# A two-batch gated cross-attention block on one core: the order of five instruction queues is written anew

## The reference, cut to what matters

```python
def _L0_xattn_ref(x1, x2, x1_scale, x1_zp, x2_scale, x2_zp):
    q1 = fake_quant(x1, x1_scale, x1_zp)     # clip(round(x/s + z), 0, 255), then (q - z) * s
    q2 = fake_quant(x2, x2_scale, x2_zp)
    return jnp.matmul(q1, q2)                # (2, 1024, 2048) x (2, 2048, 2048)

def _L0_ffn_ref(x, route_w, A, Bw):          # 8 experts of rank 16, top 1
    logits = jnp.einsum('bsd,ed->bse', x, route_w)
    topk_v, topk_idx = jax.lax.top_k(logits, 1)
    route_weight = jax.nn.one_hot(topk_idx[..., 0], E) * topk_v
    h = jnp.einsum('bsd,erd->bser', x, A)
    return jnp.einsum('bser,eor->bso', route_weight[..., None] * h, Bw)

x = x + jnp.tanh(g_xattn[0]) * _L0_xattn_ref(_layernorm(x), ctx_4096, ...)
x = x + jnp.tanh(g_ffn[0]) * _L0_ffn_ref(_layernorm(x), route_w, A, Bw)
```

## Time and profile before

| what | value |
|---|---|
| median of 3 runs | 368.99 us (368.56 to 371.08) |
| profiled execution, its own time | 369.88 us |
| its span, first to last instruction | 367.8 us (2.08 lie outside) |
| mean granted TensorE clock | 0.996 |
| TensorE busy | 336.4 us, 91% |
| VectorE / ScalarE / GpSimd busy | 262.0 / 197.2 / 174.0 us |
| main queue's DMA (q1) | 87.11 MB, 80.3% of 16 engines |

### The profile page before, as it was taken

How to read it: one execution, slowest core, us unless ns; L and a number is a source line. 1 busy time by engine, 2 the same in 40 slices (tenths; PEclk the granted TensorE clock), 3 DMA queues, 4 the chain that set the end, 5 groups by cost and what they waited for, 6 DMA issues and landing times.

```text
span 367.8 us, 5879 instructions
## 1 busy us (share of the span) xinstructions
PE 336.4 (91%) x2262; PEld 187.0 (51%) x2262; DVE 262.0 (71%) x553; ACT 197.2 (54%) x129; POOL 174.0 (47%) x199
## 2 busy tenths in 40 slices
PE   0249999999999989999999999999999999999983
PEld 0124544555666644645564645555465546464851
DVE  3899784698876984879539688775885768365853
ACT  1699589458994382282999554406054305104360
POOL 2386649501207534137799537425426181505281
PEclk9999999999999999999999999999999999999998
DMA  7999989959768969997699997578919864913836
GB/s 309 398 365 386 396 326 313 342 223 362 244 215 218 220 229 168 401 344 161 174 262 253 218 367 150 155 145 317 199 26 279 215 124 82 211 44 58 268 134 228
DMA packets 93906, 87.63 MB, mean 238 GB/s; under 512 B 71844, under 2 KB 72868, under 8 KB 89764
## 3 DMA queue, kind: packets, MB, share of 16 engines
q1 hardware_dynamic: 93856, 87.11, 80.3%
q10 hardware_dynamic: 12, 0.00, 0.0%
HBM read 52.49 MB, written 16.78 MB: 188 GB/s over the span
## 4 chain that ended last, share of the span: by engine, by line
PE 61%; DMA 12%; DVE 9%; ACT 8%; issue 4%; POOL 3%; SPq 1%; ACTq 0%; DVEq 0%
PE main L1575 39%; DMA stage<-in_ctx 7%; ACT c L735 3%; DMA xs<-in_x 3%; DVE bn L971 3%; PE hp L1617 3%; PE outp L1658 3%; PE outp L1660 3%; PE outp L1659 3%; PE hp L1614 3%; PE hp L1613 3%; DMA prow<-in_g_ffn 2%; PE turn L1503 1%; ACT yn L782 1%; POOL yn L586 1%
## 5 line engine op out<-in xcount | busy, mean ns | idle before, releaser
L1575 PE MATMUL main<-q,qa 128*128 128x512 bf16 x864 | 196.8, 382 | 1.2 <-POOL q L593 0.8
L1575 PEld LDWEIGHTS main<-q,qa 128*128 128x128 bf16 x864 | 83.4, 98 | 100.1 <-issue 2.9
L586 POOL TENSOR_TENSOR yn<-y,yn 128x2048 f16<-128x2048 f32 x13 | 53.0, 4079 | 31.5 <-ACT y L788 31.2
L735 ACT ACTIVATE c<-stage,zpc,inv 128x2048 int8<-128x2048 f32 x24 | 49.7, 2088 | 19.5 <-DMA stage<-in_ctx 19.3
L1104 DVE SCALAR_TENSOR_TENSOR xs<-main,cc,xs 128x512 f32<-128x512 f32 x45 | 33.5, 744 | 31.2 <-PE main L1575 30.6
L593 POOL CAST q<-c 128x2048 bf16<-128x2048 int8 x24 | 45.1, 1900 | 9.1 <-ACT c L735 8.7
L574 POOL TENSOR_SCALAR ve<-mv 128x1 f32<-128x1 f32 x16 | 3.1, 192 | 91.3 <-DVE mv L1137 87.3
L793 ACT ACTIVATE whT<-wp 128x256 f16<-128x256 f16 x16 | 6.1, 379 | 67.5 <-PE wp L1646 67.5
L971 DVE BATCH_NORM_STATS2 bn<-xs 128x6 f32<-128x512 f32 x52 | 32.0, 678 | 10.9 <-DMA xs<-in_x 10.9
L1184 DVE SCALAR_TENSOR_TENSOR xs<-outp,tsc,xs 128x512 f32<-128x512 f32 x44 | 31.1, 736 | 11.5 <-PE outp L1660 11.4
L1613 PE MATMUL hp<-WT,yT 128*128 128x136 f16 x256 | 34.8, 223 | 0.0
(11 more groups left out here) (132 smaller groups left out, 440.4 us busy)
## 6 DMA issues: line engine op xcount, KB each, us to landing
stage<-in_ctx SPq DMA_DIRECT2D x24, 1024.0 KB, 7.7
xs<-in_x SPq DMA_DIRECT2D x13, 1024.0 KB, 6.4
out<-xs SPq DMA_DIRECT2D x12, 1024.0 KB, 4.9
yT<-in_ctx SPq DMA_DIRECT2D x4, 1024.0 KB, 11.2
y<-in_ctx SPq DMA_DIRECT2D x4, 1024.0 KB, 11.4
c<-in_x SPq DMA_DIRECT2D x3, 1024.0 KB, 8.3
out<-c SPq DMA_DIRECT2D x3, 1024.0 KB, 5.1
c<-in_L_ffn_A SPq DMA_DIRECT2D x1, 1024.0 KB, 16.7
```

The costliest lines, as they stand in the source:

```text
L586: pool.tensor_tensor(yn[:, 1, :], y[:, :], yn[:, 0, :], ALU.subtract).then_inc(s_ylo_made, 1)
L735: act.activation(c8_of(piece), place(piece), ACT.Identity, bias=zpc[:, 1:2], scale=inv[:, 1:2])\
L1575: last = pe.matmul(bank_of(n)[:, :], q1T(t)[:, k, :], q2[:, nb, k, :], start=(k == 0), stop=(k == KC - 1))
```

## The change

The five written-out lists get a new order; functions, buffers, semaphores and their counts, `RAMP`, `HOME` and the split between engines stay. The same calls are made, each as often as before. What moves: x2 loads behind pieces 0 and 1, x3, A and the router behind pieces 4 to 7 (before: behind 1 and 3); in blocks 0 and 1 the runs of tiles 0 to 2 go piece by piece over several tiles, instead of unit by unit; tile 3's transposes come after those 24 runs. From there to the end many neighbours in each list change places. The core of the diff, in the order SyncE, GpSimd, ScalarE, VectorE, TensorE:

```diff
             load_x(0)
             load_x(1)
-            load_x(2)
             load_ctx(0)
             load_ctx(1)
-            load_x(3)
+            load_x(2)
             load_ctx(2)
             load_ctx(3)
-            load_a()
-            load_router()
             load_ctx(4)
             load_ctx(5)
             load_ctx(6)
             load_ctx(7)
+            load_x(3)
+            load_a()
+            load_router()
+            load_ctx(8)
             load_x(4)
-            load_ctx(8)
             load_ctx(9)
...
             flip_high(3)
+            flip_low(3)
             load_x(6)
-            flip_low(3)
+            load_ctx(25)
             store(1)
-            store(2)
             flip_high(4)
             flip_low(4)
+            store(2)
+            load_ctx(26)
             load_x(7)
-            load_ctx(26)
             load_ctx(27)
+            flip_high(5)
             store(3)
+            flip_low(5)
+            load_x(8)
             load_ctx(28)
-            load_x(8)
             load_ctx(29)
-            flip_high(5)
-            flip_low(5)
-            store(4)
             flip_high(6)
             flip_low(6)
             flip_q1(8)
+            store(4)
+            load_ctx(30)
             load_x(9)
-            load_ctx(30)
             load_ctx(31)
...
             store(7)
-            load_x(13)
-            load_x(14)
             flip_high(10)
             flip_low(10)
             flip_q1(12)
+            load_x(13)
+            load_x(14)
...
             first_norm(0)
             first_norm(1)
-            first_norm(2)
             widen_ctx(0)
             widen_ctx(1)
-            first_norm(3)
+            first_norm(2)
             widen_ctx(2)
...
+            second_norm(6)
             first_norm(8)
-            second_norm(6)
+            low_rows(6)
             widen_x(8)
-            low_rows(6)
             widen_ctx(16)
...
+            affine_first(0)
             affine_first(1)
-            affine_first(0)
+            affine_ctx(0)
             affine_x(1)
-            affine_ctx(0)
             affine_ctx(1)
+            affine_ctx(2)
             affine_x(2)
-            affine_ctx(2)
             affine_ctx(3)
-            affine_x(3)
             affine_ctx(4)
-            mult_a()
             affine_ctx(5)
             affine_ctx(6)
             affine_ctx(7)
+            affine_x(3)
+            mult_a()
             affine_ctx(8)
...
             norm_full(2)
+            affine_x(5)
             take_wh(0)
-            affine_x(5)
...
             take_q1T(0, 0)
+            take_q1T(0, 1)
             see_q1(0)
-            stats1(2)
-            take_q1T(0, 1)
             widen_x(1)
             see_q1(1)
-            stats1(3)
-            widen_x(2)
+            stats1(2)
             take_q1T(1, 0)
             take_q1T(1, 1)
-            scale_a()
-            scale_router()
+            widen_x(2)
+            take_q1T(2, 0)
+            take_q1T(2, 1)
+            see_q1(2)
             unit_terms(0, 0)
...
+            add_main(2, 0)
...
+            stats1(3)
+            scale_a()
+            widen_x(3)
+            see_q1(3)
             take_q1T(3, 0)
             take_q1T(3, 1)
+            add_main(0, 1)
+            scale_router()
             take_a(0)
...
+            add_main(3, 2)
             take_b(0)
             take_b(1)
+            unit_terms(0, 3)
             take_b(2)
             take_b(3)
-            add_main(3, 2)
-            unit_terms(0, 3)
             scale_b()
             add_main(0, 3)
...
+            add_experts(3, 0)
             take_q1T(6, 1)
...
+            stats1(7)
             add_experts(3, 1)
...
+            gate(6)
+            add_experts(5, 0)
             stats1(9)
-            gate(6)
             tile_terms(8)
             add_main(8, 0)
...
+            stats1(13)
+            stats1(14)
             tile_terms(12)
-            add_experts(8, 3)
+            add_main(12, 0)
...
             stats2_sum(15)
+            add_experts(12, 1)
+            norm_group(15, 0)
+            norm_group(15, 2)
             add_experts(12, 2)
-            norm_group(15, 0)
             add_experts(12, 3)
-            norm_group(15, 2)
             gate(14)
...
             turn_q1(0, 0)
             turn_q1(0, 1)
+            main(0, 0, 0)
             turn_q1(1, 0)
             turn_q1(1, 1)
-            column_sums(0, [0])
-            main(0, 0, 0)
+            main(0, 0, 1)
+            main(1, 0, 0)
+            main(1, 0, 1)
+            main(0, 0, 2)
+            main(1, 0, 2)
             turn_q1(2, 0)
             turn_q1(2, 1)
-            main(0, 0, 1)
...
+            main(1, 1, 0)
+            main(1, 1, 1)
+            main(2, 1, 0)
+            main(2, 1, 1)
+            main(1, 1, 2)
+            main(2, 1, 2)
+            main(0, 1, 0)
+            main(0, 1, 1)
+            main(0, 1, 2)
...
             turn_q1(3, 0)
             turn_q1(3, 1)
             turn_a(0)
-            column_sums(0, [1])
-            main(0, 1, 0)
-            main(0, 1, 1)
+            main(3, 0, 0)
+            main(3, 1, 0)
+            main(3, 1, 1)
             turn_a(1)
...
             turn_y(15, 2)
             h_group(15, 0)
+            h_group(15, 1)
+            turn_y(15, 3)
             expert_product(14, 0)
-            turn_y(15, 3)
             expert_product(14, 1)
-            h_group(15, 1)
```

More of the change, by code:

```diff
@@ L453, in _ @@
             load_ctx(18)
+            load_x(5)
             load_ctx(19)
-            load_x(5)
             load_ctx(20)
@@ L522, in _ @@
             flip_low(14)
+            store(10)
             store(11)
@@ L632, in _ @@
             widen_ctx(11)
-            widen_x(4)
+            first_norm(4)
             widen_ctx(12)
@@ L637, in _ @@
             widen_ctx(15)
+            widen_x(4)
             second_norm(0)
@@ L863, in _ @@
             affine_ctx(16)
+            affine_x(4)
             affine_ctx(17)
@@ L891, in _ @@
             norm_full(4)
+            affine_ctx(24)
+            affine_ctx(25)
+            take_wh(3)
             affine_x(6)
-            affine_ctx(24)
-            take_wh(3)
-            affine_ctx(25)
+            norm_high(5)
+            norm_full(5)
             affine_ctx(26)
+            affine_x(7)
             affine_ctx(27)
-            norm_high(5)
             take_wh(4)
-            affine_x(7)
-            norm_full(5)
-            affine_x(8)
             norm_high(6)
             norm_full(6)
+            affine_x(8)
             widen_ctx(18)
@@ L934, in _ @@
             norm_high(11)
+            norm_full(11)
             affine_x(13)
-            norm_full(11)
+            affine_x(14)
             take_wh(10)
-            affine_x(14)
             norm_high(12)
             norm_full(12)
+            affine_x(15)
             take_wh(11)
@@ L943, in _ @@
             norm_full(13)
-            affine_x(15)
             take_wh(12)
@@ L1338, in _ @@
             add_main(5, 1)
+            add_experts(2, 2)
+            add_experts(2, 3)
+            gate(4)
             add_main(5, 2)
+            add_main(5, 3)
             take_q1T(6, 0)
+            stats2_sum(5)
+            tile_terms(6)
+            add_experts(3, 0)
             take_q1T(6, 1)
-            add_main(5, 3)
-            stats2_sum(5)
-            add_experts(3, 0)
+            stats1(7)
             add_experts(3, 1)
@@ L1366, in _ @@
             add_main(7, 1)
+            add_experts(4, 1)
+            add_experts(4, 2)
+            add_experts(4, 3)
             add_main(7, 2)
@@ L1423, in _ @@
             add_experts(9, 1)
-            add_experts(9, 2)
-            add_experts(9, 3)
-            add_main(12, 0)
-            add_main(12, 1)
             add_main(12, 2)
@@ L1430, in _ @@
             stats2_sum(12)
+            add_experts(9, 2)
+            add_experts(9, 3)
             tile_terms(13)
@@ L1756, in _ @@
             main(2, 3, 2)
-            main(2, 3, 3)
+            spread_scales()
+            turn_q1(4, 0)
+            turn_q1(4, 1)
             turn_y(0, 0)
             turn_y(0, 1)
+            main(2, 3, 3)
+            h_group(0, 0)
             column_sums(3, [3])
+            turn_y(0, 2)
+            turn_y(0, 3)
             main(3, 3, 0)
@@ L1795, in _ @@
             expert_product(0, 3)
+            h_rows_high(2)
+            turn_q1(5, 0)
+            main(4, 2, 3)
+            h_rows_low(2)
             turn_wh(1)
-            h_rows_high(2)
-            h_rows_low(2)
-            main(4, 2, 3)
-            expert_product(1, 0)
             main(4, 3, 0)
@@ L1882, in _ @@
             main(7, 3, 1)
+            expert_product(4, 3)
+            turn_wh(5)
             main(7, 2, 2)
@@ L1938, in _ @@
             h_rows_low(8)
+            expert_product(7, 2)
             column_sums(10, range(NB))
             main(10, 0, 0)
+            main(10, 1, 0)
+            main(10, 1, 1)
```

(18 more changed lines are left out.)

451 lines of the change are left out of this document (199 added, 252 removed).

## The result

The changed kernel takes **364.05 us** (median of 3 runs, 363.53 to 364.25) against 368.99: a ratio of 0.987, 95% interval 0.9844 to 0.9897. In another set of runs it was 363.46 us, ratio 0.9869 (0.9849 to 0.9888). The gain, 4.8 to 4.9 us or 1.3%, is more than the 1.3 us forecast. The time lies inside the range, 0.4 us above its lower end and 0.15 us from what rival R1 (the lead is kept) gave. So some 1.2 us of the traces' 6.1 are scatter between executions; the kept traces do not show where it arises.

A forecast was written before the change was run, and what follows sets the result against it. TensorE bounds it, improvable only in start, tail and 3.2 us of idle time. Start lead 5.3 us, 1.85 left at tile 8, 0.7 after x9, plus 0.6 in the tail: 368.99 - 1.3 = 367.7 us; range 363.6 to 371.8.

The forecast's parts named there:

- R1: Rival, the lead is kept: x3, x7 and x9 land 2 us sooner, 3.8 us more gained, 363.9; chance 0.2.
- (a): Tile 3's transposes: cast held behind x3's statistics and A's maximum on VectorE; TensorE waits 0.9 us.
- (g): Tile 7's statistics stand before add_experts(3,1), load_x(7) issued near 146; TensorE waits 1.4 us at expert_product(3,3).
- (f): At 133.00: today's 1.17 us wait for add_experts behind tile 6's statistics falls away.
- (d): add_main(0,3) behind four takes of B and B's maximum on VectorE: ready 81.3 against 80.6, 0.8 us lost.
- x9: Tile 9's load comes after store(4), behind flip_q1(8); add_main(8,0) late, TensorE waits 0.6 to 3.8 us, 1.5 taken.
- (b): Piece 11 lands at 54.5 and is wide at 58.4; TensorE waits 0.35 us.
- (c): B, as load 23, lands at 69.7 and is permuted at 71.6; TensorE waits 0.9 us.
- (e): take_wh(0) now behind norm_full(2) and affine_x(5) on ScalarE: 0.5 us lost.
- R2: Rival, x9 behind the store: slower once flip_q1(8) starts after about 182.5; 370.0, or 374.2 with a slow transpose; chance 0.18.
- R3: Rival, slow TensorE clock: if all six scattered start runs are slow, 1.5 us lost, 369.2; chance 0.22 together with R4.
- R4: Rival: ScalarE and DMA set the start's pace, lead 0 by tile 0's transposes; 368.6; chance 0.22 together with R3.

The follow-up runs named there:

- e5: Changed kernel with tile 3 of x loaded and normed ahead of piece 7 and expert_product(4,3) two runs earlier: 362.73 us, ratio 0.9848 to before.
- e1b: Start only: the change's orders up to and with piece 11, behind it the orders of the kernel before: 368.56 us, ratio 0.9990 to before.
- e7: The change's orders up to B's transposes and piece 18, behind that those of the kernel before: 366.27 us, ratio 0.9938 to before.
- e8: e1b with tile 4's ScalarE pass behind pieces 12 to 16 and B's permutation, its GpSimd widening behind piece 15's: 365.47 us, ratio 0.9911 to before.
- e2: Rest only: before's orders up to the end of the first 24 runs, the change's behind: 369.23 us, ratio 1.0019 to before.
- e6: Kernel before, loads included, with TensorE's first 24 runs piece by piece and tile 2's transposes moved up on VectorE: 375.35 us, ratio 1.0176 to before.
- e11: Changed kernel with tile 9's statistics on VectorE moved behind add_main(8,0) and add_main(8,1): 364.31 us, ratio 0.9881 to before.
- e9: e7 with tile 0's second norm and first two transposed quarters ahead of pieces 19 and 20 on ScalarE: 369.32 us, ratio 1.0017 to before.
- e1: Start only: the change's orders up to the end of the first 24 runs, cut ahead of piece 11, before's behind: 374.66 us, ratio 1.0179 to before.
- e3: Changed kernel with TensorE taking the first 24 runs unit by unit instead of piece by piece: 366.60 us, ratio 0.9957 to before.

## Why the prediction was too small

**The number.** I forecast 367.7 us and the time is 364.05, 3.65 lower; "one or two us gained" (chance 0.4) did not come, "faster by more than 1%" (chance 0.18) did. The range holds it because of R1 (chance 0.2), whose condition did not come true as I had put it, so that the 0.15 us to R1's 363.9 are luck. None of my three signs of being wrong appeared either: they did not guard against the error that I made.

**The start: right, 0.7 us under-sized.** The landing times of loads 12 and 13 were good: x3 at 36.4 and A at 39.4 in my list, their first uses on VectorE at 36.20 and 39.35. Piece 2 was ready for TensorE at 24.73, not 25.65. The dense stretch came 0.95 us before my 28.8, and the run count was right.

**The give-backs: the steps (a) to (g) sum to 3.7 us lost; they measured 0.9 us gained** (0.60 lost at (a), 1.17 back at (f), 0.3 back at (d)). My sum took 3.45 for them: its "roundings" of 0.2 have no term behind them. Measured, that makes 6.0 + 0.9 - 1.1 for x9 = 5.8 us, where the lead in work done is 6.1 at tile 8 and at the gates; 0.3 is not accounted for. Term by term, in VectorE's and ScalarE's timelines of the changed kernel:

```profile
36.20 2.47 DVE L971 BATCH_NORM_STATS2 bn<-xs 128x6 f32<-128x512 f32 x4 [0.44 <-DMA xs<-in_x]
...
39.35 2.29 DVE L1025 TENSOR_REDUCE wmax<-c 128x1 f32<-128x2048 f32 x1 [0.38 <-DMA c<-in_L_ffn_A]
...
42.88 1.23 DVE L1007 CAST q<-x 128x2048 bf16<-128x2048 int8 x1 [0.86 <-ACT x L753]
```

```profile
47.29 2.09 ACT L735 ACTIVATE c<-y,zpc,inv 128x2048 int8<-128x2048 f32 x1 [0.53 <-DMA y<-in_ctx]
50.00 2.09 ACT L735 ACTIVATE c<-stage,zpc,inv 128x2048 int8<-128x2048 f32 x1 [0.62 <-DMA stage<-in_ctx]
52.71 2.09 ACT L735 ACTIVATE c<-stage,zpc,inv 128x2048 int8<-128x2048 f32 x1 [0.62 <-DMA stage<-in_ctx]
...
66.58 1.91 ACT L809 ACTIVATE xs<-c 128x2048 f32<-128x2048 f32 x1 [0.71 <-DMA c<-in_L_ffn_Bw]
```

- (a) 0.9 forecast, 0.60 measured. A's maximum is not on the path: the cast waits 0.86 us for ScalarE behind it, and e5 took the wait away by x3's load alone.
- (b) 0.35 against 0, (c) 0.9 against 0. **This is the step that failed.** I let the nth load land at 3.03n and carried that to B, load 23. A line through zero was the error: the first load is used only at 5.75, and the tenth is taken at 30.36, which is 2.73 us per load. From the tenth to the thirteenth it is 3.05, and that made 3.03n fit both of the places at which I looked. After the change pieces 9, 10 and 11 (loads 16 to 18), each taken on its landing, are 2.71 apart, and B is taken 13.87 us and five loads later, 2.77 each: at 66.58, where I had it landing at 69.7. Both rows were there to be read. (The DMA share of "above 0.9" that I gave with it holds for the first 28.66 us; piece 7, at 39.51, lies in the stage that reads 0.89.) As to the mechanism of (c) it was no invention: where B's permutation stands behind 2 us more of ScalarE (e1b), it costs 3.45 us and the clock.
- (d) 0.8 against 0.27 at main(2,3,0), plus 0.43 at turn_y(0,0), which I had not listed; against them two waits of before fell away, 0.83 at turn_y(0,0) for ScalarE's norm and 0.20 near 105, so 0.3 gained. In the trace of before:

```profile
89.84 1.09 PE L1609 MATMUL turn<-idf,y 128*128 128x128 f32 x8 [0.83 <-ACT y L762]
...
104.79 1.26 PE L1609 MATMUL turn<-idf,y 128*128 128x128 f32 x8 [0.20 <-DVE yT L1142]
```

- (e) 0.5 against 0: no wait of TensorE between 84 and 193 us. (f) 1.17 back, as forecast; e1b, e7 and e8, with before's order there, have 0.9 to 1.2 us of that wait, and in e2, with the change's, it is gone.
- (g) 1.4 against 0. load_x(7) is issued at 141.85, not 146, and VectorE takes tile 7 from 147.05 on without a wait. A store can leave when its tile is done, so its time moves with the lead; by giving (a) to (e) back first I had moved it late, and each later step counted that delay over again.
- x9: 1.5 forecast, 1.42 measured, at main(8,2,0), with VectorE 2.39 us idle for it. The chain is right; the size is a pick near the lower end of my 0.6 to 3.8, and the place in time moved with the lead. One link I had missed: the queue is free of flip_q1(8) at 177.50, but store(4) leaves at 178.66, since the change has moved expert_product(4,3) behind main(7,3,1) and VectorE waits for it:

```profile
177.88 0.75 DVE L1184 SCALAR_TENSOR_TENSOR xs<-outp,tsc,xs 128x512 f32<-128x512 f32 x1 [1.96 <-PE outp L1660]
```

The wait did not absorb any of the lead, since every link from the experts of tile 4 on came earlier with TensorE. e5 put that product two runs sooner: the store leaves at 177.07 and the wait is gone.
- Tail: 0.6 to be gained by forecast, 0 measured. The gate of tile 14 is 6.08 us earlier than before, that of tile 15 6.09.

**The account.** The spans differ by 6.1 us where I had 1.3. Of the 4.8 between, (g) is 1.4, (d) 1.1, (c) 0.9, the start 0.7, (e) 0.5, (b) 0.35, (a) 0.3 and x9 0.1, less the 0.6 of the tail: 4.75. (g) came out of the same error, since it rests on the lead that (a) to (e) had taken away. Some 1.2 us of the 4.8 are scatter between executions, which is why the medians miss the forecast by 3.65 only.

**The rivals.** R1 held in its result and not in its condition. x3 landed where I had it; x7 and x9 came 4 us sooner and more, but with the lead, and x9's wait stayed. The start's extra 0.7 and the steps (b) to (e) made up for that. R2's decision point (flip_q1(8) after 182.5) was never near: it starts at 174.85. R3: the four matmuls at 16.95 and the sixteen transposes at 18.61 are at the slow pace, the eleven at 21.11 no longer (2.55 us; 10 x 0.216 + 0.38 = 2.54), so one run of the six is slow. The slow stretch opened where TensorE had idled 5.7 us, and did not come back over waits of 0.58 and 1.07. R4 is ruled out by the lead of 6.1 at tile 8.

**The port pair.** x1's and x2's casts both read 1.23 us, x2's 2.60 before, so they fell between GpSimd's casts as forecast; in e6 tile 2's and tile 3's casts (26.92 and 42.34) fall beside GpSimd's, and read 2.50 and 2.88. That agrees with the rule of the Trainium skill (SBUF — State Buffer, "SBUF: two separate sides").

**What I did not ask at all** was whether the later orders were needed. I held each later move to be a cost or nothing. e1b and e2 show the opposite: they are what lets the lead pass.

## What to carry to other kernels

A lead won in one stage passes only through queues that were laid out for it: test such a change as start alone, rest alone and both, since here 0 and 0 made 4.8 us. When you step through a new order by hand, let every store and load move with the lead before you charge a wait, or each step counts the last one's error again; and take a load's spacing from the difference between two landings, never from one landing divided by its number. A wait is gone only if the thing behind it in the queue has slack: e11 and e9 moved one and got another.

## What the runs showed of the hardware

- **A long wait of TensorE costs more than its length.** After 3.45, 6.77 and 9.57 us of waiting the granted clock of the next 5 to 6 us was 0.50, 0.50 and 0.62, in e1b, e9 and e1; it had fallen before the wait was over (0.87, 0.69 and 0.68 in it). In e1b's profiled execution that was 2.7 us on top of 3.45. After waits of 2.48 (e7) and 1.62 (e8) in an otherwise dense stretch it stayed at 1.00. Where TensorE had had gaps before, shorter waits came with a fall as well: after 2.58 us in the start of e3, 7.80 us read 0.78; after 3.82 us in e6, 6.73 us read 0.58. The Trainium skill (TensorE: Matmul & The Clock Gate, "What's actually happening") says that idleness throttles; the trace agrees, with these numbers.
- **Loads of 1 MB landed some 2.7 us apart, from the first to the twenty-third:** 2.73 from the first to the tenth before, 2.71 at the sixteenth to eighteenth and 2.77 on to the twenty-third in the changed kernel. The DMA engines moved 385 to 387 GB/s between 15 and 30 us and 386 to 388 between 45 and 60, and at 387 a load of 1.049 MB takes 2.71 us. Around the twelfth and thirteenth load it was more (3.05 before, 3.15 from x3 to A after). No run tells why.
- **The issue of a DMA transpose on SyncE's queue has no fixed length.** That of tile 9 held the queue for 4.81 us when issued at 199.39 in the changed kernel, and for 1.84 when issued at 202.54 in e11: 3.1 us later in, 0.2 later out, and TensorE waits for it in neither. This is the slack that I had missed.
